# The Linear stage of a cross-attention and fp8 feed-forward kernel: rounding from a magnitude that ScalarE makes, with three fused VectorE operations per tile

## What is computed

```python
def _quant_e4m3(t):
    amax = jnp.max(jnp.abs(t)).astype(jnp.float32)
    scale = jnp.maximum(amax / E4M3_MAX, 1e-12)
    fp8 = (t.astype(jnp.float32) / scale).astype(jnp.float8_e4m3fn)
    return (fp8, scale)

def _scaled_mm(a_fp8, b_fp8, sa, sb):
    acc = jnp.matmul(a_fp8.astype(jnp.float32), b_fp8.astype(jnp.float32))
    return (acc * (sa * sb)).astype(jnp.bfloat16)

x = x + _L0_xattn_ref(_layernorm(x, axis=-1), ctx_512, Wq, Wkv_expand, Wout)   # attention stage
x = x + _L0_ffn_ref(_layernorm(x, axis=-1), L0_ffn_weight)                     # Linear stage
```

## Time and profile before

| what | us |
|---|---|
| median of the 3 runs | 2032.49 |
| the runs | 2031.47 to 2033.93 |
| span of the profiled execution | 2032.3 |
| attention stage and what comes ahead of it, to the last of its matmuls | about 1684 |
| DVE in the Linear stage, from the end of the first r to the end of the last | 318.86 |
| from the end of the last r to the end of the span | 14.1 |

### The profile page before, as it was taken

The page is one execution under the profiler, slowest core; times in us unless marked ns, Lnnn a source line. Parts: engine busy times, 40 slices in busy tenths (PEclk is TensorE's granted clock), DMA queues, the critical chain, the costliest instruction groups (busy, mean ns, idle before and its releaser), DMA issues.

```text
span 2032.3 us, 29487 instructions
## 1 busy us (share of the span) xinstructions
PE 1903.7 (94%) x11368; PEld 971.8 (48%) x11368; DVE 1487.2 (73%) x1869; ACT 713.3 (35%) x668; POOL 232.0 (11%) x146
## 2 busy tenths in 40 slices
PE   6699999999999999999999999999999995888777
PEld 3444554545445544554555445545545542333333
DVE  6766677567666766676667666765779877999997
ACT  6421133113221321232223212311332225777775
POOL 1000000000000000000000000000000202555555
PEclk9899999999999999999999999999999997999999
DMA  9531112221222122222212212221222113555554
GB/s 305 161 104 62 62 64 78 62 72 54 78 66 88 53 59 83 73 63 68 73 63 64 78 62 63 66 75 62 63 63 63 43 51 145 212 204 204 206 206 155
DMA packets 105559, 196.91 MB, mean 97 GB/s; under 512 B 56320, under 2 KB 58880, under 8 KB 104960
## 3 DMA queue, kind: packets, MB, share of 16 engines
q1 hardware_dynamic: 105472, 195.59, 29.9%
HBM read 119.28 MB, written 71.30 MB: 94 GB/s over the span
## 4 chain that ended last, share of the span: by engine, by line
PE 77%; issue 9%; POOL 8%; DVE 3%; ACT 1%; SPq 0%; DMA 0%; POOLq 0%; DVEq 0%; ACTq 0%
PE ps_o L566 32%; PE ps_s L566 32%; POOL tile_space L484 8%; PE ps_p L575 3%; PE ps_x L575 2%; PE ps_x L556 2%; PE ps_p L556 2%; DVE m_buf L951 1%; PE ps_p L545 1%; PE ps_p L546 1%; PE ps_x L545 0%; DVE n_buf L951 0%; PE ps_x L546 0%; DVE wo_t L1130 0%; ACT m_buf L756 0%
## 5 line engine op out<-in xcount | busy, mean ns | idle before, releaser
L566 PE MATMUL ps_s<-m_buf,tile_space 128*128 128x512 f16 x3072 | 685.3, 380 | 2.5 <-DVE tile_space L951 2.5
L566 PE MATMUL ps_o<-n_buf,tile_space 128*128 128x512 f16 x3072 | 681.6, 379 | 3.6 <-DVE tile_space L951 1.9
L566 PEld LDWEIGHTS ps_s<-m_buf,tile_space 128*128 128x128 f16 x3072 | 301.2, 98 | 355.2 <-issue 7.1
L566 PEld LDWEIGHTS ps_o<-n_buf,tile_space 128*128 128x128 f16 x3072 | 296.1, 98 | 342.1 <-DVE n_buf L951 3.5
L951 DVE SCALAR_TENSOR_TENSOR tile_space<-ps_p,tile_space 128x1024 f16<-128x1024 f32 x64 | 78.4, 1224 | 317.3 <-ACT tile_space L756 316.8
L756 ACT ACTIVATE tile_space<-ps_p 128x1024 f16<-128x1024 f32 x64 | 65.5, 1024 | 464.5 <-PE ps_p L575 464.5
L459 POOL TENSOR_TENSOR rstd_x<-veps_x,minus_half 128x1 f32<-128x1 f32 x64 | 35.5, 554 | 1511.1 <-DVE veps_x L972 1511.1
L484 POOL TENSOR_TENSOR tile_space<-tile_space 128x1024 f32<-128x1024 f32 x64 | 178.7, 2792 | 157.2 <-ACT tile_space L865 157.2
L756 ACT ACTIVATE tile_space<-ps_x 128x1024 f16<-128x1024 f32 x64 | 65.5, 1024 | 276.8 <-PE ps_x L575 276.8
L772 ACT ACTIVATE tile_space<-tile_space,neg_mean 128x1024 f32<-128x1024 f32 x64 | 73.5, 1148 | 242.7 <-DVE neg_mean L1029 242.7
L997 DVE TENSOR_REDUCE hmax<-ps_s 128x16 f32<-128x1024 f32 x64 | 78.3, 1223 | 64.7 <-PE ps_s L566 64.4
(11 more groups left out here) (156 smaller groups left out, 2103.8 us busy)
## 6 DMA issues: line engine op xcount, KB each, us to landing
tile_space<-in_x_dram SPq DMA_DIRECT2D x128, 512.0 KB, 3.9
x_scratch<-tile_space SPq DMA_DIRECT2D x64, 512.0 KB, 4.8
tile_space<-x_scratch SPq DMA_DIRECT2D x64, 512.0 KB, 3.7
out_dram<-tile_space SPq DMA_DIRECT2D x64, 512.0 KB, 2.7
m_buf<-in_L_xattn_Wq_dram SPq DMA_DIRECT2D x4, 1024.0 KB, 10.9
n_buf<-in_L_xattn_Wout_dram SPq DMA_DIRECT2D x2, 2048.0 KB, 18.3
tile_space<-_L_xattn_Wkv_expand_dram SPq DMA_DIRECT2D x4, 512.0 KB, 10.4
wq_stack<-wo_t SPq DMA_DIRECT2D x8, 256.0 KB, 6.3
```

Source lines behind the costliest of these rows:

```text
L566: mm = nc.tensor.matmul(to[:, cols], left[:, ls, c * P:(c + 1) * P], right[:, rs, c, cols], start=(c == 0 and i == 0), stop=(c == CT - 1 a ...
```

## The change

ACT writes the magnitude |v| times (2^20 - 4), with the function Abs, for every tile (`magnitudes`), and v no longer. DVE uses that magnitude itself in place of the power of two g: per tile three scalar_tensor_tensor, v = x * a + b (`values`, with b as a tensor of one column that is broadcast over the row), a = max(u, least) + v (`shifted`) and r = max(u, least) - a (`rounded`). The exponent mask (`constant_g`) is gone. There are four buffers for u, two for v, two for a; and sixteen `x2` buffers, the first eight in `m_buf`, which the attention stage no longer needs by then. SP stores tile t and then reloads the buffer of tile t - 1. The loop bodies now cover sixteen tiles.

```diff
 ROUND_SHIFT = 2.0 ** 20
+ROUND_UNDER = 2.0 ** 20 - 4.0
...
-        X2 = 8
-        x2 = [tile_space[:, i, :] for i in range(X2)]
+        X2 = 16
+        x2_m = flat(m_buf).bitcast(F32).rearrange("p (i h) -> p i h", h=H)
+        x2 = [x2_m[:, i, :] for i in range(8)] + [tile_space[:, i, :] for i in range(8)]
...
-            def values(t, i, e, first):
+            def magnitudes(t, i, k, first=False):
                 act.wait_ge(got_x1[i], (t - i) * (16 // X2) + 16)
                 if not first:
-                    act.wait_ge(g_done, t - 1)
-                nc.scalar.activation(u_t[e], x2[i], ACT.Identity, bias=quant_b20[:, bass.ds(t, 1)],
+                    act.wait_ge(r_ready, t - 3)
+                nc.scalar.activation(u_t[k], x2[i], ACT.Abs, bias=quant_b20[:, bass.ds(t, 1)],
                                      scale=quant_a20[:, bass.ds(t, 1)]).then_inc(u_ready, 1)
-                if e == 0 and not is_step(t, 0):
-                    if not first:
-                        act.wait_ge(a_done, t - 1)
-                    nc.scalar.activation(v_t[e], x2[i], ACT.Identity, bias=quant_b[:, bass.ds(t, 1)],
-                                         scale=quant_a[:, bass.ds(t, 1)]).then_inc(v_ready, 1)
...
             def step2(t, i, first=False):
-                e, ahead = i % 2, (i + 5) % X2
+                e, ahead = i % 2, (i + 4) % X2
                 scaled(t, e, first)
                 copy_rt(t + 2, e, False)
-                values(t + 5, ahead, ahead % 2, False)
+                magnitudes(t + 4, ahead, ahead % 4)
...
-                nc.vector.tensor_scalar(g_t[e].bitcast(U32), u_t[e].bitcast(U32), EXPONENT_BITS, HALF_BIT,
-                                        ALU.bitwise_and, ALU.bitwise_or).then_inc(g_done, 1)
-
-            def value_v(t, i, first=False):
+            def values(t, i, e, first=False):
                 dve.wait_ge(got_x1[i], (t - i) * (16 // X2) + 16)
                 if not first:
                     dve.wait_ge(a_done, t - 1)
-                nc.vector.tensor_scalar(v_t[1], x2[i], quant_a[:, bass.ds(t, 1)], quant_b[:, bass.ds(t, 1)], ALU.mult,
-                                        ALU.add).then_inc(v_odd, 1)
+                nc.vector.scalar_tensor_tensor(out=v_t[e], in0=x2[i], scalar=quant_a[:, bass.ds(t, 1)],
+                                               in1=quant_b[:, bass.ds(t, 1)].to_broadcast([P, H]), op0=ALU.mult,
+                                               op1=ALU.add).then_inc(v_ready, 1)
+
+            def shifted(t, e, k, first=False):
+                dve.wait_ge(u_ready, t + 1)
+                dve.wait_ge(v_ready, t + 1)
+                if not first:
+                    dve.wait_ge(r_ready, t - 1)
+                nc.vector.scalar_tensor_tensor(out=a_t[e], in0=u_t[k], scalar=ROUND_LEAST, in1=v_t[e], op0=ALU.max,
+                                               op1=ALU.add).then_inc(a_done, 1)
...
-                nc.vector.scalar_tensor_tensor(out=r_t[e], in0=g_t[e], scalar=ROUND_LEAST, in1=a_t[e], op0=ALU.max,
+                nc.vector.scalar_tensor_tensor(out=r_t[e], in0=u_t[k], scalar=ROUND_LEAST, in1=a_t[e], op0=ALU.max,
                                                op1=ALU.subtract).then_inc(r_ready, 1)
...
+            def quantise(t, i, first=False, last=False):
+                shifted(t, i % 2, i % 4, first)
+                if not last:
+                    values(t + 1, (i + 1) % X2, (i + 1) % 2, is_step(t, 0))
+                rounded(t, i % 2, i % 4, first)
```

More of the change, by code:

```diff
@@ L236, in xattn_ffn_kernel @@
         quant_ready = sem("quant_ready")
-        g_done = sem("g_done")
         a_done = sem("a_done")
-        got_x1 = [sem(f"got_x1_{i}") for i in range(8)]
+        got_x1 = [sem(f"got_x1_{i}") for i in range(16)]
         u_ready = sem("u_ready")
         v_ready = sem("v_ready")
-        v_odd = sem("v_odd")
         r_ready = sem("r_ready")
@@ L248, in xattn_ffn_kernel @@
         sum_ready = sem("sum_ready")
-        out_stored = [sem(f"out_stored{i}") for i in range(8)]
+        out_stored = [sem(f"out_stored{i}") for i in range(16)]
         wq_flat = wq_stack[:].rearrange("p h c -> p (h c)")
@@ L410, in load_x1, with store_out, reload @@
                 sp.dma_start(x2[i], x1_dram[bass.ds(t * P, P), :]).then_inc(got_x1[i], 16)
-            for t in range(4):
+            def store_out(t, i):
+                sp.wait_ge(sum_ready, t + 1)
+                sp.dma_start(out_rows[bass.ds(t * P, P), :], x2[i]).then_inc(out_stored[i], 16)
+            def reload(q, i):
+                sp.wait_ge(out_stored[i], q * 16 + 16)
+                load_x1((q + 1) * X2 + i, i)
+            sp.wait_ge(s_full, T)
+            for t in range(8):
                 load_x1(t, t)
@@ L416, in _ @@
             sp.wait_ge(x1_done, T)
-            for t in range(4, X2):
+            for t in range(8, X2):
                 load_x1(t, t)
-            def store_out(t, i):
-                sp.wait_ge(sum_ready, t + 1)
-                sp.dma_start(out_rows[bass.ds(t * P, P), :], x2[i]).then_inc(out_stored[i], 16)
+            store_out(0, 0)
             with sp.Fori(0, T // X2 - 1) as q:
-                for i in range(X2):
+                for i in range(1, X2):
                     store_out(q * X2 + i, i)
[L427 to L431, removed]
+                    reload(q, i - 1)
+                store_out((q + 1) * X2, 0)
+                reload(q, X2 - 1)
+            for i in range(1, X2):
                 store_out(T - X2 + i, i)
@@ L867, in _ @@
             act.wait_ge(quant_ready, 1)
[L868 to L869 removed]
+            for t in range(4):
+                magnitudes(t, t, t, True)
             for t in range(2):
                 copy_rt(t, t, True)
[L872 removed]
             def step2(t, i, first=False):
[L875 removed]
+                e, ahead = i % 2, (i + 4) % X2
                 scaled(t, e, first)
                 copy_rt(t + 2, e, False)
[L878 to L881 removed]
+                magnitudes(t + 4, ahead, ahead % 4)
+            for t in range(2):
+                step2(t, t, True)
             with act.Fori(0, T // X2 - 1) as q:
[L883 removed]
+                for i in range(2, 2 + X2):
                     step2(q * X2 + i, i % X2)
[L885 to L888, removed]
+            for t in range(T - X2 + 2, T):
+                if t + 4 < T:
+                    step2(t, t % X2)
+                else:
+                    scaled(t, t % 2, False)
+                    if t + 2 < T:
+                        copy_rt(t + 2, t % 2, False)
         @block.vector
@@ L1183, in _ @@
             nc.vector.tensor_scalar(small[:, 8:9], small[:, 6:7], small[:, 4:5], None, ALU.mult).then_inc(dve_step, 1)
-            nc.vector.tensor_scalar(quant_a20, quant_a[:], ROUND_SHIFT, None, ALU.mult).then_inc(dve_step, 1)
+            nc.vector.tensor_scalar(quant_a20, quant_a[:], ROUND_UNDER, None, ALU.mult).then_inc(dve_step, 1)
             steps[0] += 2
             dve.wait_ge(dve_step, steps[0])
[L1187 to L1193, removed]
-                nc.vector.tensor_scalar(g_t[e].bitcast(U32), u_t[e].bitcast(U32), EXPONENT_BITS, HALF_BIT,
-                                        ALU.bitwise_and, ALU.bitwise_or).then_inc(g_done, 1)
-            def value_v(t, i, first=False):
+            nc.vector.tensor_scalar(quant_b20, quant_b[:], ROUND_UNDER, None, ALU.mult).then_inc(quant_ready, 1)
+            def values(t, i, e, first=False):
                 dve.wait_ge(got_x1[i], (t - i) * (16 // X2) + 16)
@@ L1248 @@
+            dve.wait_ge(quant_ready, 1)
+            values(0, 0, 0, True)
+            for t in range(2):
+                quantise(t, t, True)
+            with dve.Fori(0, T // X2 - 1) as q:
+                for i in range(2, 2 + X2):
+                    quantise(q * X2 + i, i % X2)
+            for t in range(T - X2 + 2, T):
+                quantise(t, t % X2, last=(t == T - 1))
 _INS = ['x', 'ctx_512', 'L0_xattn_Wq', 'L0_xattn_Wkv_expand', 'L0_xattn_Wout', 'L0_ffn_weight']
```

24 lines of the change are left out of this document (3 added, 21 removed).

## The result

The changed kernel takes **2048.06 us** (median of 4 runs, 2045.07 to 2048.62), the kernel before 2033.21 on the same occasions. The ratio is 1.0072, with a 95% interval of 1.006 to 1.0084: 14.9 us slower. Forecast were 2045.8 us and a loss of 13.3. One of the four runs of e2_one_sbuf_input took 2035.58 us at a lower granted clock (0.937, against 0.986 to 0.987 in the others), so its time is the median of the other three.

What follows compares the result with a forecast made beforehand. DVE was taken to bound the Linear stage: its own pitches plus 1.88 us per POOL addition. Span 2032.3 + 12.1 (stretch) + 0.6 (before first r) + 0.6 (head pause) = 2045.6, median 0.2 above: 2045.8 us; range 2031 to 2056.

Steps and rivals of the forecast that it cites:

- The bound: Linear stage: DVE sets the pace, its time being its own pitches plus 1.88 us for each POOL addition.
- The fused operation stands still too: Linear stage: a fused DVE operation with both tensors in SBUF and a POOL addition exclude each other, 1.89 us lost each.
- Rival A: Linear stage: fused operations run free of POOL, 4.1 us a tile, 1972 us; chance 0.12 together with its milder form.
- its milder form: Linear stage: only v, with its one-column broadcast operand, runs free of POOL; about 4.2 us a tile, 1977 us; within Rival A's 0.12.
- The floor of 4.1 us a tile: Linear stage under Rival A: limit by the round from r through y to the u three tiles on, also PE's need.
- The meeting point: Linear stage: POOL asks 0.10 us after an r ends, waits for the a, then blocks the v; 5.33 us a tile.
- Rival B: Linear stage: POOL loses to gapless fused operations and runs only when DVE stops; 6.1 us a tile, 2093 us; chance 0.07.
- v bare: Linear stage: pitch of an unblocked fused v, taken as 1.18 us, range 1.13 to 1.24.
- A blocked v: Linear stage: a fused v held up by POOL's addition has a pitch of 3.07 us, losing 1.89.
- rival C: Linear stage: the bare cost is smaller than thought, the sum shrinks to +2 us, 2034 us; chance 0.06.
- the pause at the head: Before the fifth a: DVE idles 2.5 us for u, POOL's first addition no longer blocks (-1.9); net +0.6 us.
- the step from a span to a median: Whole kernel: the median of the runs lies 0.2 us above the profiled span.

Runs made afterwards that it cites:

- e2_one_sbuf_input: Changed kernel with v and a sharing one PSUM buffer, v a tensor_scalar into PSUM, one SBUF input per DVE operation; 1974.19 us.
- e1: Changed kernel with v alone taken back from the fused operation to a tensor_scalar, for every tile; 2013.63 us, 0.9902 of the kernel before.
- e4: Changed kernel in which POOL adds y to only 512 of the 1024 columns; 1987.79 us, 0.9772 of the kernel before.
- e5: e2_one_sbuf_input with each of DVE's three operations cut into two halves of 512 columns; 1960.9 us, 0.964 of the kernel before.
- e7: e2_one_sbuf_input with POOL adding y to only 512 of the 1024 columns; 1973.48 us, 0.9702 of the kernel before.

## Why the prediction was right, point by point

**The bound.** DVE was full before and after, and e1, e2, e4 and e5 each moved the time by moving DVE's: 4.81, 4.15, 4.36 and 3.90 us a tile where the changed kernel has 5.34.

**The fused operation stands still too.** This was the step on which the sign hung, and it rested on two rows of before. Now 58 of 64 v show it, and e4 and e7 show the mechanism from both sides. Rival A, that fused operations run free of POOL, falls, and its milder form with it: a fused operation whose second tensor is one broadcast column is blocked like the others. The floor of 4.1 us a tile that I gave rival A, as what PE needs, was too high too: PE does a tile in 3.90 in e5.

**The meeting point.** Forecast: POOL asks 0.10 us after the end of an r, which is 0.18 into the a, waits for the a, and blocks the v, 5.33 us a tile. Measured: 0.09 to 0.17 into the a in 58 of the 64 additions (the others are the first three and the last three), v blocked, 5.34. Rival B needed POOL to lose against a fused operation that follows without a gap. It never did: the v is issued about 0.1 us before the end of the a (1881.80 against 1881.88), POOL has asked since 1880.76, and POOL goes first. The rule of the Trainium skill that I had set beside it ("SBUF — State Buffer", "Who interferes with whom": the order of issue decides, and the later one stands still for the whole instruction) agrees with these rows, and with e4, where POOL came 0.07 us ahead of the v and the v lost.

**The terms.** v bare: forecast 1.18; at the head of the changed kernel the pitch is 1.19, from the two rows below. A blocked v 3.07: measured 3.07. With that rival C, a smaller bare cost, falls too.

```profile
1698.49 1.28 DVE L1199 SCALAR_TENSOR_TENSOR n_buf<-m_buf,quant_a,quant_b 128x1024 f32<-128x1024 f32 x1
...
1699.68 1.22 DVE L1217 SCALAR_TENSOR_TENSOR tile_space<-n_buf 128x1024 bf16<-128x1024 f32 x1
```

The stretch from the first r to the last: forecast 330.9 and 0.6 for the pause at the head, measured 331.74 (but see below: two small misses offset each other). Up to the first r: forecast 0.6 more, measured 0.5 (1692.49 to 1697.43, 4.94 us, against 1694.87 to 1699.35, 4.48). The tail: 14.1 us in both.

**What was off.** The pause before the fifth a. I took ACT's first y from the trace of before, 10.0 us after the first r; here it came 8.1 after, at 1705.51:

```profile
1706.71 3.11 POOL L491 TENSOR_TENSOR m_buf<-m_buf,tile_space 128x1024 f32<-128x1024 f32 x1 [15.77 <-ACT tile_space L867]
1707.42 1.24 ACT L854 ACTIVATE n_buf<-m_buf,ident 128x1024 f32<-128x1024 f32 x1
1708.69 2.21 DVE L1209 SCALAR_TENSOR_TENSOR n_buf<-n_buf 128x1024 f32<-128x1024 f32 x1 [0.86 <-ACT n_buf L854]
```

DVE idled 0.86 us and not 2.5, and then its a still stood behind the rest of POOL's addition (2.21 us for 1.21). Together that is what one block costs anyway, so the term is about 0 and not 0.6. The 0.8 us that the stretch has above 330.9 come from elsewhere: a tile takes 5.34 and not 5.33, which over 61 additions is 0.6, and the rest I have not traced. That the sum with the 0.6 lies within 0.2 us of the measured stretch is in part luck.

The other one is the step from a span to a median. The profiled execution of the changed kernel has a span of 2043.3 us, 11.0 more than before and not 13.3, because everything ahead of the Linear stage, which the change does not touch, was 2.4 us shorter in it (ACT's first u at 1692.49 against 1694.87). It was the fastest of the four runs; the median lies 3 us higher. The profiles of the experiments scatter in the same way: the first r ends between 1697.81 and 1700.31. (The table of before puts the end of the attention stage's last matmul at about 1684; in its trace that is 1679.0.) So the part that the change touches grew by 13.3 us as forecast, and the medians say 14.9; the 1.6 between them is less than the 3.5 us by which the four runs differ.

## What to carry to other kernels

Before swapping a short VectorE operation for another kind, look not only at its bare length but at what it does when GpSimd works beside it: a pair of engines that exclude each other costs nearly the sum of both, and a full VectorE row can hide a third of standing still (3.76 us of 10.22 before, 1.88 of 5.34 after). Compare the maximum of a line with its median; a few long instances of an operation tell what it will do when it is always the one that meets GpSimd. If such a pair sets the pace, try PSUM: one input of each VectorE operation that reads two tensors, and the output of the tensor_scalar. Here that took GpSimd's whole work off VectorE's path, and the kernel fell from 2033 to 1974 us, the gain of the missing mask included.

## What the runs showed of the hardware that I had not expected

- What the fused v loses when it is blocked is GpSimd's length less about 0.25 us, at 512 columns (1.15 and 0.90) as at 1024 (2.12 and 1.88). What comes out the same is the blocked pitch: about 3.07 us for every fused operation at 1024 columns, whether it is 1.13 or 1.19 bare, and 2.54 for a tensor_scalar, whether it is 0.61 or 0.72 bare. So the loss itself ranges from 1.82 to 1.94.
- With its output in PSUM a tensor_scalar of 1024 float32 takes 1347 ns, against 0.81 us with the output in SBUF, and is not held up by GpSimd at all (e5 has the v that start inside an addition). Next to an addition of 2.1 us the slower form is the cheaper one: it takes 1.35 us where the fast one took 2.62.
- Six VectorE instructions on halves, each independent of the one ahead, took 3.90 us, and three on whole tiles that wait for each other 4.15. Half as long is not half the price (two a 1.20 us of pitch against one of 1.13), but the waits between dependent ones were dearer.
